# Latent attention in head pairs: PSUM banks assigned by kind of work, weight splitting and quotients moved from VectorE to ScalarE and GpSimd, reciprocals spread over the steps

## The chip, the core and the metric

One core of one Trainium2 chip runs a kernel of two transformer layers (linear attention, mixture of experts, latent attention, a quantised feed-forward). The metric is the device time of one execution in microseconds. TensorE (PE) has its own weight loads (PEld), VectorE is DVE, ScalarE is ACT, GpSimd is POOL, SyncE (SP) issues most DMAs. All engines run their own instruction lists in order and wait for each other on semaphores.

## The reference, cut to the stage that is changed

```python
# _L1_attn_ref: b=2, s=1024 (the shape in use), H=16 heads, NOPE, ROPE, VD = 128, 64, 128, LORA=64
q = (x @ wq).reshape(b, s, H, QH).transpose(0, 2, 1, 3)
kva = x @ wkv_a
ckv, k_pe = (kva[..., :LORA], kva[..., LORA:])
ckv = ckv * rsqrt(mean(ckv * ckv) + EPS) * kv_norm_scale
kv = (ckv @ wkv_b).reshape(b, s, H, NOPE + VD).transpose(0, 2, 1, 3)
k_nope, v = (kv[..., :NOPE], kv[..., NOPE:])
q_pe, k_pe = _rope(q_pe, cos, sin), _rope(k_pe, cos, sin)
scores = einsum('bhqd,bhkd->bhqk', qs, ks_) * QH ** -0.5      # causal
attn = softmax(scores, axis=-1)
out = einsum('bhqk,bhkd->bhqd', attn, v).transpose(0, 2, 1, 3).reshape(b, s, H * VD)
return out @ wo
```

## The kernel before, in words

**What a core holds.** Key and value weights are folded into the query and output weights beforehand, so all heads share one key tile `k_hl` (64 latent rows and 64 rotated rows, 128 x 1024) and one value tile `v_hl` (64 latent columns, 64 columns of ones). Every fp32 operand is split into a high and a low fp32r part (`_hl`), and a product is three matmuls: high by high, high by low, low by high. The PSUM tensor `bank` (`all_bank` in the rows) has eight banks of 128 x 512 fp32.

**Loops.** `phase_attention` (L1230) runs once per batch entry, twice in all. It goes over 8 head pairs n, and within a pair over 10 groups x = 0 to 9. A group is a block i of 256 queries (both heads side by side, 512 columns) and a pair jj of key tiles, jj <= i: block 0 is x=0, block 1 is x=1, 2, block 2 is x=3 to 5, block 3 is x=6 to 9. One pass of the loop over u (L1414), that is one group, is called a step; u counts steps over all pairs. Each engine has its own loop over the same steps.

**A step on TensorE** (L1414 to L1431): first half of the scores of step u+2, one aside item, second half of those scores, an aside item, first half of the values of step u, an aside item, second half of the values, any further item. `scores` (L1358) writes two banks, alternating between banks 0, 1 and 2, 3. `values` (L1382) accumulates over a block; block e uses bank 4 or 5 by turns, and the first values of a block wait until the block before the last has been copied out (`sums_sb`, L1388).

**Aside items** belong mostly to the next pair. A *query* (L1331, Q0 to Q3, one in each of x=0 to 3) is six matmuls that make 128 query rows x 512 tokens. A *piece* (L1346) is the scores of 128 queries of one head against up to 512 keys; VectorE takes its row maximum (`peaks`, L1568), which `spread` (L1574) turns into the diagonal matrix `minus` that the scores subtract. There are three pieces in most steps from x=4 on. All aside items share banks 6 and 7 in turn (`bank_of`, L1305), in the order of one list, so each waits until the reader of the item two places before it is through (`bank_free`, L1321): `by_cos` after a query, `peaks` after a piece. The aside list in x=0 is query, piece, piece; in x=1 query, piece; in x=2 query, piece; in x=3 query, piece, piece.

**What a query needs behind it.** ScalarE swaps halves of the rotated rows (`swap`, L1435, two copies out of PSUM), VectorE multiplies by the cosines (`by_cos`, L1559, out of PSUM into `raw`), GpSimd multiplies the swapped rows by the sines (L1510) and adds (L1513; the two are `rotate`), ScalarE makes the high part (`q_high`, L1450), GpSimd the low part (`q_low`, L1520).

**ScalarE's order in a step** (L1490): swap, `probs` (the exponential, L1457) and `highs` (L1464) of step u+2, `q_high`, and, where a block ends, `sums` (four copies of 64 x 256 out of the value bank, L1475 and L1476). **GpSimd's order** (L1538): `q_low` of the query before, `rotate`, `low` of step u+2 (the low part of the probabilities, L1526). **VectorE's order** (L1616): the readers of the step's aside items (where the step has a query, the first piece goes ahead of it), then the quotients of a block (`divide`, L1589: two reciprocals of 128 x 128, L1596, two products, L1600) in steps 2, 4, 7 and 1 of the next pair, then the splitting of the weights of the pair after next: `weights_high` (L1553) in step 5, `weights_low` (L1557) in step 6. SyncE loads those weights (L1317) when the splitting before is through.

**Opening and last pair.** Before the loop TensorE makes the four queries of pair 0 and 16 of its pieces (L1404 to L1413), and VectorE reads them all and splits the weights of pair 1. In the last pair there are no queries and no pieces of a next pair. The last block's quotient is taken in `phase_output`, which the change does not touch.

Of the kernel before, what the change touches and what calls it, by code (L numbers as in the profile page):

```python
# [13 lines left out]
F32 = mybir.dt.float32  # L14
# [4 lines left out]
ALU = mybir.AluOpType  # L19
# [3 lines left out]
P = 128  # L23
# [1206 lines left out]
def phase_attention(nc, name, bank, cst_turned, turned_loaded, bf, xT, x_hl, wqk_rows, w_raw, w_hl, k_hl, v_hl, oT, last_den):  # L1230
# [28 lines left out]
    DIVIDE_AT = {2: 0, 4: 1, 7: 2, 1: 3}  # L1259
# [12 lines left out]
    order = opening + [item for n in range(PAIRS) for x in range(NG) for item in aside(n, x)]  # L1272
    place = {item: a for a, item in enumerate(order)}
# [9 lines left out]
    with Memory(nc, name) as m:  # L1283
# [10 lines left out]
        rden = m.sb("rden", [P, 2, P])  # L1294
# [16 lines left out]
        with nc.Block() as block:  # L1311
# [8 lines left out]
            def _(pe):  # L1320
                def bank_free(item):  # L1321
                    a = place[item]
                    if a < 2:
                        return
                    kind, n, v = order[a - 2]
                    if kind == "query":
                        pe.wait_ge(raw_sb, n * QC + v + 1)
                    else:
                        pe.wait_ge(peak_sb, n * NP + v + 1)

                def query(item):  # L1331
                    _, n, k = item
                    h, c = chunk(k)
                    bank_free(item)
# [3 lines left out]
                    for xs, ws in ((0, 0), (0, 1), (1, 0)):  # L1338
                        for kc in range(KC):
                            mm = nc.tensor.matmul(bank_of(item), w_hl[:, ws, kc, h * P:(h + 1) * P],  # L1340
# [41 lines left out]
                def values(u, half):  # L1382
# [9 lines left out]
                    out = pv_ps[e % 2].rearrange("p (h m) -> p h m", h=2)[:, :, q0:BW]  # L1392
# [41 lines left out]
            def _(act):  # L1434
                def swap(n, k):  # L1435
                    c = n * QC + k
                    ps = bank_of(("query", n, k))
# [3 lines left out]
                    nc.scalar.copy(swapped[LORA:LORA + 32, c % 2], ps[LORA + 32:P])  # L1441
                    nc.scalar.copy(swapped[LORA + 32:P, c % 2], ps[LORA:LORA + 32]).then_inc(swap_sb, 1)
# [23 lines left out]
                def sums(n, i):  # L1466
# [5 lines left out]
                    for h in range(2):  # L1472
                        half, cols = slice(h * LORA, (h + 1) * LORA), slice(h * BW, (h + 1) * BW)
                        own = last_den[half, :] if e == PAIRS * NB - 1 else den[half, e % 2, :]
                        nc.scalar.copy(own, pv_ps[e % 2][LORA:P, cols])  # L1475
                        done = nc.scalar.copy(oT[half, n, i * BW:(i + 1) * BW], pv_ps[e % 2][0:LORA, cols])  # L1476
# [5 lines left out]
                for k in range(QC):  # L1482
                    q_high(0, k)
                    if k + 2 < QC:
                        swap(0, k + 2)
# [578 lines left out]
```

## Time and profile before

| What | Value |
|---|---|
| Time of three runs | 1497.5, 1510.41 (median), 1512.34 us |
| Profiled execution | 1508.22 us, of which the span from the first to the last instruction is 1506.4 us |
| TensorE clock over the span | 0.924 of full |
| Busy share of the span | PE 83%, POOL 65%, DVE 61%, PEld 59%, ACT 46% |
| First run of the attention stage | from 491 us (first query matmul) to 919 us (last copy of the value sums) |
| Second run of it | from 961 us to 1387 us |

Times inside a trace are microseconds from the start of the span. A timeline row gives start, duration, engine, line, operation, output<-input, shape and count, and in brackets the engine's idle time before it and what ended that. Where a row has a count above one, its duration is the merged stretch. A granted clock of 1.00 is 2.4 GHz and 0.50 is 1.2 GHz.

### The profile page before, as it was taken

How to read it: one execution, taken by the hardware profiler on the slowest of the kernel's cores; microseconds unless marked ns; L12 is line 12 of the kernel's file. 1: busy time of each engine (PE TensorE's matmuls, PEld its weight loads, DVE VectorE, ACT ScalarE, POOL GpSimd, SP SyncE). 2: the span in 40 equal slices, each digit the busy share in tenths (PEclk: the TensorE clock that was granted, in tenths of full speed). 3: DMA queues.
4: the chain of work that ended last, by engine and by line, in shares of the span. 5: the costliest groups of instructions: out<-in, count | busy, mean ns of one | idle time of the engine just before them, and what ended most of it. 6: DMA issues, size and time to landing. Idle time of an engine off the chain costs nothing. (4 is left out here: it accounts for less than half of the span.)

```text
span 1506.4 us, 19134 instructions
## 1 busy us (share of the span) xinstructions
PE 1245.2 (83%) x5880; PEld 883.6 (59%) x5881; DVE 911.9 (61%) x1575; ACT 692.3 (46%) x1183; POOL 984.2 (65%) x688
## 2 busy tenths in 40 slices
PE   6965699999954788988988897688889888988797
PEld 5854455555533456655655576556556556666786
DVE  4578422222217467686768675556867777775557
ACT  3211233333312366556656664255666566657242
POOL 2017588888855577678767755766776677676554
PEclk9976699999985699999999999889999999999899
DMA  9367245555443000000000000000000000001101
GB/s 326 122 181 171 80 79 83 79 81 80 80 77 127 14 1 8 8 8 1 8 8 1 1 1 12 8 8 8 7 1 8 8 1 8 0 1 38 25 8 49
DMA packets 66512, 68.31 MB, mean 45 GB/s; under 512 B 15072, under 2 KB 59680, under 8 KB 66304
## 3 DMA queue, kind: packets, MB, share of 16 engines
q1 hardware_dynamic: 48336, 43.42, 9.8%
q0 software_dynamic: 15168, 20.72, 8.7%
q10 hardware_dynamic: 2928, 3.15, 0.6%
q8 instruction: 44, 0.72, 0.2%
q14 instruction: 36, 0.29, 0.1%
HBM read 46.17 MB, written 21.10 MB: 45 GB/s over the span
## 5 line engine op out<-in xcount | busy, mean ns | idle before, releaser
L1526 POOL TENSOR_TENSOR att_prob_lo<-att_prob,att_prob_hi 128x1024 fp32r<-128x1024 f32 (+1 forms) x160 | 351.8, 2199 | 202.3 <-ACT att_prob_hi L1464 202.3
L1571 DVE TENSOR_REDUCE att_peak<-all_bank 128x1 f32<-128x512 f32 (+3 forms) x384 | 205.8, 552 | 199.8 <-PE all_bank L1355 138.5
L1371 PE MATMUL all_bank<-att_q_hl,sequence_k_hl 128*128 128x512 f32 (+1 forms) x960 | 272.9, 396 | 0.0
L1352 PE MATMUL all_bank<-sequence_k_hl,att_q_hl 128*128 128x512 f32 (+3 forms) x384 | 184.5, 484 | 84.3 <-DVE all_xT L1565 63.0
L1457 ACT ACTIVATE att_prob<-all_bank 128x1024 f32<-128x1024 f32 (+1 forms) x160 | 150.5, 941 | 196.3 <-PE all_bank L1377 165.0
L1394 PE MATMUL all_bank<-att_prob_hi,sequence_v_hl 128*128 128x512 f32 (+1 forms) x640 | 206.0, 403 | 2.3 <-POOL att_prob_lo L1526 2.0
L1371 PEld LDWEIGHTS all_bank<-att_q_hl,sequence_k_hl 128*128 128x128 f32 x960 | 176.8, 199 | 27.9
L1464 ACT CAST att_prob_hi<-att_prob 128x1024 fp32r<-128x1024 f32 (+1 forms) x160 | 153.9, 962 | 5.2
L916 PE MATMUL all_bank<-early_w_gu,moe_xgT 128*128 x316 | 148.8, 553 | 3.5 <-issue 2.4
L1352 PEld LDWEIGHTS all_bank<-sequence_k_hl,att_q_hl 128*128 128x128 f32 x384 | 78.3, 205 | 123.3 <-DVE all_xT L1565 78.1
L881 POOL DMA_INDIRECT sums<-moe_y,early_slot_far x79 | 125.5, 1589 | 36.4 <-issue 18.5
L1340 PE MATMUL all_bank<-sequence_x_hl,sequence_w_hl 128*128 128x512 f32 x384 | 112.4, 432 | 34.0 <-DVE all_xT L1565 26.3
L1394 PE MATMUL all_bank<-att_prob_lo,sequence_v_hl 128*128 128x512 f32 x320 | 121.5, 380 | 0.0
L1377 PE MATMUL all_bank<-att_minus,all_bf 128*128 128x512 bf16 x320 | 120.1, 375 | 0.0
L1394 PEld LDWEIGHTS all_bank<-att_prob_hi,sequence_v_hl 128*128 128x128 f32 x640 | 111.0, 196 | 12.7 <-POOL att_prob_lo L1526 4.1
L1600 DVE TENSOR_TENSOR late_oT<-late_oT,att_rden 128x128 f32<-128x128 f32 x124 | 115.0, 966 | 0.0
L1596 DVE RECIPROCAL att_rden<-att_den 128x128 f32<-128x128 f32 x124 | 108.6, 916 | 10.5 <-ACT late_oT L1476 10.5
L1008 DVE COPY moe_hidT<-all_bank 112x256 f32<-112x256 f32 x79 | 33.6, 425 | 123.6 <-PE all_bank L926 123.6
L1340 PEld LDWEIGHTS all_bank<-sequence_x_hl,sequence_w_hl 128*128 128x128 f32 x384 | 73.7, 198 | 57.8 <-DVE all_xT L1565 35.9
L871 POOL DMA_INDIRECT moe_xg<-x_rows,early_slot_row x79 | 84.2, 1065 | 26.1 <-issue 21.5
L1513 POOL TENSOR_TENSOR all_xT<-all_xT 128x512 f32<-128x512 f32 x64 | 82.3, 1286 | 25.4 <-DVE all_xT L1565 18.0
L935 PE MATMUL all_bank<-early_w_down,moe_hidT 112*128 x316 | 87.3, 399 | 13.6 <-issue 12.2
(246 smaller groups left out, 2197.8 us busy)
## 6 DMA issues: line engine op xcount, KB each, us to landing
sequence_w_raw<-wqk_rows SPq DMA_DIRECT2D x16, 256.0 KB, 2.7
early_w_gu<-in_gate SPq DMA_DIRECT2D x16, 224.0 KB, 5.7
early_w_gu<-in_up SPq DMA_DIRECT2D x16, 224.0 KB, 5.9
early_w_down<-in_down SPq DMA_DIRECT2D x1, 3584.0 KB, 19.4
sums<-early_zero SPq DMA_DIRECT2D x18, 128.0 KB, 3.9
all_xT<-in_xT SPq DMA_DIRECT2D x4, 512.0 KB, 7.6
all_x_tok<-in_x SPq DMA_DIRECT2D x1, 2048.0 KB, 16.2
x_rows<-all_x_tok SPq DMA_DIRECT2D x4, 512.0 KB, 3.0
```

The costliest lines, as they stand in the source:

```text
L881: nc.gpsimd.indirect_dma_start(sums[s], bass.IndirectOffsetOnAxis(slot_far[:, r:r + 1], 0), y[:, s, :], None, bounds_check=last_far, compu ...
L916: mm = nc.tensor.matmul(gu_ps[s], xgT[:, s, k, :], w_gu[:, bass.ds(e * (KC * 2 * I) + k * 2 * I, 2 * I)], start=k == 0, stop=k == KC - 1)
L1340: mm = nc.tensor.matmul(bank_of(item), w_hl[:, ws, kc, h * P:(h + 1) * P], x_hl[:, xs, kc, c * WIDE:(c + 1) * WIDE], start=i == 0, stop=i ...
L1352: mm = nc.tensor.matmul(ps[:, 0:w], q_hl[n % 2][:, 0, h, t * P:(t + 1) * P], k_hl[:, 0, k0:k0 + w], start=True, stop=not diagonal)
L1371: nc.tensor.matmul(ps, k_hl[:, ks, j * P:(j + 1) * P], q_hl[n % 2][:, qs, :, i * BW + q0:(i + 1) * BW], start=g == 0, stop=False)
L1377: mm = nc.tensor.matmul(ps, bf["ones"], minus[:, i, :].rearrange("p (h m) -> p h m", h=2)[:, :, q0:BW], start=False, stop=True)
L1394: mm = nc.tensor.matmul(out, v_hl[:, vs, j, :], part[:, u % 3, half * WIDE:half * WIDE + 2 * w].rearrange("p (h m) -> p h m", h=2), start= ...
L1457: nc.scalar.activation(prob[:, u % 2, 0:w], s_ps[u % 2][:, 0:w], ACT.Exp, scale=SCALE).then_inc(prob_sb, 1)
L1464: nc.scalar.copy(prob_hi[:, u % 3, 0:w], prob[:, u % 2, 0:w]).then_inc(hi_sb, 1)
L1526: nc.gpsimd.tensor_tensor(prob_lo[:, u % 3, 0:w], prob[:, u % 2, 0:w], prob_hi[:, u % 3, 0:w].bitcast(F32), ALU.subtract).then_inc(lo_sb, 1)
L1571: nc.vector.tensor_reduce(peak[:, n % 2, part, t // 2, h, t % 2:t % 2 + 1], bank_of(("piece", n, y))[:, 0:w], AX_X, ALU.max).then_inc(peak ...
L1600: nc.vector.tensor_tensor(own, own, rden[:, half, :], ALU.mult).then_inc(o_sb, 1)
```

## The change

TensorE's aside items no longer share two banks. Queries have bank 5 alone, and each waits for the cosine product of the query before it. Pieces alternate between banks 6 and 7, each waiting for the maximum two pieces before. The value sums have bank 4 alone, so the first values of a block wait for the copies of the block just before. The high part of the weights is made by ScalarE in step 4, the low part by GpSimd in step 5. `divide` is gone: VectorE takes one reciprocal of 128 x 128 in each of steps 1 to 8, and GpSimd one product of 128 x 256 in steps 3, 5, 7 and 9.

```diff
-    DIVIDE_AT = {2: 0, 4: 1, 7: 2, 1: 3}
+    INVERT_AT = {1: (-1, 0), 2: (-1, 1), 3: (0, 0), 4: (0, 1), 5: (1, 0), 6: (1, 1), 7: (2, 0), 8: (2, 1)}
+    PRODUCT_AT = {3: -1, 5: 0, 7: 1, 9: 2}
...
-        rden = m.sb("rden", [P, 2, P])
+        rden = m.sb("rden", [P, 2, BW])
...
-        pv_ps = [bank[:, n, :] for n in (4, 5)]
-        aside_ps = [bank[:, n, :] for n in (6, 7)]
-
-        def bank_of(item):
-            return aside_ps[place[item] % 2]
+        pv_ps, q_ps = bank[:, 4, :], bank[:, 5, :]
+        piece_ps = [bank[:, n, :] for n in (6, 7)]
...
                 def query(item):
-                    bank_free(item)
+                    if n * QC + k:
+                        pe.wait_ge(raw_sb, n * QC + k)
...
                 def piece(item):
-                    bank_free(item)
+                    if n * NP + y >= 2:
+                        pe.wait_ge(peak_sb, n * NP + y - 1)
                     pe.wait_ge(q_hi_sb, n * QC + t // 4 * 2 + h + 1)
-                    ps = bank_of(item)
+                    ps = piece_ps[y % 2]
...
                 def values(u, half):
-                        if jj == 0 and e >= 2:
-                            pe.wait_ge(sums_sb, e - 1)
+                        if jj == 0 and e >= 1:
+                            pe.wait_ge(sums_sb, e)
...
             def _(act):
+                def weights_high(n):
+                    act.wait_ge(w_loaded, 16 * n)
+                    act.wait_ge(q_mm, n * QC)
+                    nc.scalar.copy(w_hl[:, 0], w_raw[:]).then_inc(w_hi_sb, 1)
...
                         q_high(n + 1, x)
                     if x in last_of:
                         sums(n, last_of.index(x))
+                    if x == 4 and n + 2 < PAIRS:
+                        weights_high(n + 2)
...
             def _(pool):
+                def weights_low(n):
+                    pool.wait_ge(w_hi_sb, n)
+                    nc.gpsimd.tensor_tensor(w_hl[:, 1], w_raw[:], w_hl[:, 0].bitcast(F32), ALU.subtract).then_inc(w_sb, 1)
+
+                def product(e):
+                    n, i = divmod(e, NB)
+                    own = oT[:, n, i * BW:(i + 1) * BW]
+                    pool.wait_ge(rden_sb, 2 * (e + 1))
+                    nc.gpsimd.tensor_tensor(own, own, rden[:, e % 2], ALU.mult).then_inc(o_sb, 1)
...
                     if u + AHEAD < STEPS:
                         low(u + AHEAD)
+                    if x == 5 and n + 2 < PAIRS:
+                        weights_low(n + 2)
+                    if x in PRODUCT_AT and n * NB + PRODUCT_AT[x] >= 0:
+                        product(n * NB + PRODUCT_AT[x])
...
             def _(dve):
-                def weights_high(n):
-                def weights_low(n):
-                def divide(n, i):
-                    for half in range(2):
-                        nc.vector.reciprocal(rden[:, half, :], den[:, e % 2, half * P:(half + 1) * P]).then_inc(rden_sb, 1)
-                    for half in range(2):
-                        own = oT[:, n, i * BW + half * P:i * BW + (half + 1) * P]
-                        nc.vector.tensor_tensor(own, own, rden[:, half, :], ALU.mult).then_inc(o_sb, 1)
+                def invert(e, half):
+                    cols = slice(half * P, (half + 1) * P)
                     dve.wait_ge(sums_sb, e + 1)
+                    if e >= 2 and half == 0:
+                        dve.wait_ge(o_sb, e - 1)
+                    nc.vector.reciprocal(rden[:, e % 2, cols], den[:, e % 2, cols]).then_inc(rden_sb, 1)
...
-                weights_high(1)
-                weights_low(1)
...
-                    if x in DIVIDE_AT:
-                    if x == 5 and n + 2 < PAIRS:
-                        weights_high(n + 2)
-                    if x == 6 and n + 2 < PAIRS:
-                        weights_low(n + 2)
+                    if x in INVERT_AT:
+                        i, half = INVERT_AT[x]
+                        if n * NB + i >= 0:
+                            invert(n * NB + i, half)
```

In the opening, `weights_high(1)` stands behind the four `q_high` on ScalarE, and `weights_low(1)` behind the four `q_low` on GpSimd. The readers of the query bank (`swap`, `by_cos`) and of the value bank (`sums`) take the new bank names.

## Rows read from the trace of the kernel before

**Rows 1.** Busy time by stretch: first attention stage, two pairs, two microseconds

```profile
core 0: us, PE busy (x) PEld busy (x) DVE busy (x) ACT busy (x) POOL busy (x), PEclk, DMA share, GB/s
530.00:917.00 387.00, 340.09 (x1596) 234.65 (x1596) 278.25 (x380) 240.86 (x360) 276.19 (x161) 0.97 0.02 4
630.10:681.95 51.85, 45.17 (x215) 31.19 (x213) 38.72 (x52) 32.00 (x49) 37.17 (x23) 0.97 0.02 6
681.95:732.70 50.75, 43.81 (x215) 30.24 (x213) 38.95 (x52) 32.00 (x49) 37.66 (x23) 1.00 0.02 6
758.00:760.00 2.00, 2.00 (x6) 1.10 (x5) 0.00 (x0) 0.62 (x1) 2.00 (x2) 0.50 0.03 8
```

**Rows 2.** TensorE waits, 530:917, then 985:1386 (total us, times, longest)

```profile
PE all_bank L1352 <- DVE all_xT L1565: 24.6, 15, 2.7
PE all_bank L1340 <- DVE all_xT L1565: 12.7, 12, 1.1
PE all_bank L1352 <- DVE att_peak L1571: 8.5, 20, 0.9
...
PE all_bank L1352 <- DVE all_xT L1565: 25.3, 16, 2.7
PE all_bank L1352 <- DVE att_peak L1571: 9.7, 23, 0.9
```

**Rows 3.** Timeline of TensorE in one pair, from its Q0 on

```profile
681.95 1.74 PE L1340 MATMUL all_bank<-sequence_x_hl,sequence_w_hl 128*128 128x512 f32 x6
...
685.90 0.51 PE L1352 MATMUL all_bank<-sequence_k_hl,att_q_hl 128*128 128x512 f32 x1 [0.69 <-DVE all_xT L1565]
...
690.25 0.71 PE L1394 MATMUL all_bank<-att_prob_hi,sequence_v_hl 128*128 128x512 f32 x2
...
693.89 1.66 PE L1340 MATMUL all_bank<-sequence_x_hl,sequence_w_hl 128*128 128x512 f32 x6 [1.09 <-DVE all_xT L1565]
...
699.85 1.65 PE L1340 MATMUL all_bank<-sequence_x_hl,sequence_w_hl 128*128 128x512 f32 x6 [1.15 <-DVE all_xT L1565]
...
702.04 0.71 PE L1394 MATMUL all_bank<-att_prob_hi,sequence_v_hl 128*128 128x512 f32 x2
...
705.73 0.39 PE L1352 MATMUL all_bank<-sequence_k_hl,att_q_hl 128*128 128x256 f32 x1 [2.74 <-DVE all_xT L1565]
```

**Rows 4.** Timeline of GpSimd in the same pair

```profile
691.19 1.29 POOL L1510 TENSOR_TENSOR all_xT<-all_xT,sequence_cst_turned 128x512 f32<-128x512 f32 x1 [0.45 <-ACT all_xT L1442]
693.91 1.29 POOL L1513 TENSOR_TENSOR all_xT<-all_xT 128x512 f32<-128x512 f32 x1 [1.42 <-DVE all_xT L1565]
...
700.28 1.30 POOL L1513 TENSOR_TENSOR all_xT<-all_xT 128x512 f32<-128x512 f32 x1
```

**Rows 5.** Timeline of ScalarE in the same pair

```profile
689.56 0.36 ACT L1476 COPY late_oT<-all_bank 64x256 f32<-64x256 f32 x1
...
701.61 0.62 ACT L1450 CAST att_q_hl<-all_xT 128x512 fp32r<-128x512 f32 x1 [2.42 <-POOL all_xT L1513]
...
703.39 0.36 ACT L1476 COPY late_oT<-all_bank 64x256 f32<-64x256 f32 x1
```

**Rows 6.** Timeline of VectorE in the same pair

```profile
691.21 1.30 DVE L1580 TENSOR_TENSOR att_whole<-att_peak 128x4 f32<-128x4 f32 x1
...
695.42 3.58 DVE L1600 TENSOR_TENSOR late_oT<-late_oT,att_rden 128x128 f32<-128x128 f32 x2
```

**Rows 7.** By line: low query parts (GpSimd), weight parts (VectorE)

```profile
L1520 POOL TENSOR_TENSOR att_q_hl<-all_xT,att_q_hl 128x512 fp32r<-128x512 f32 x64 | 86.1, 1347 | 0.0
...
L1557 DVE TENSOR_TENSOR sequence_w_hl<-sequence_w_raw,sequence_w_hl 128x512 fp32r<-128x512 f32 x14 | 35.2, 2517 | 0.1
```

**Rows 8.** Timeline of the opening, VectorE

```profile
506.12 0.69 DVE L1565 TENSOR_TENSOR all_xT<-all_bank,sequence_cst_turned 128x512 f32<-128x512 f32 x1 [3.15 <-POOL att_q_hl L1520]
```

**Rows 9.** Timeline of the last pair, ScalarE and TensorE

```profile
898.87 0.37 ACT L1475 COPY att_den<-all_bank 64x256 f32<-64x256 f32 x1
...
899.11 0.71 PE L1394 MATMUL all_bank<-att_prob_hi,sequence_v_hl 128*128 128x512 f32 x2
```

More of the change, by code:

```diff
@@ L1271, in phase_attention @@
     opening = [("query", 0, k) for k in range(QC)] + [("piece", 0, y) for y in range(EARLY)]
-    order = opening + [item for n in range(PAIRS) for x in range(NG) for item in aside(n, x)]
-    place = {item: a for a, item in enumerate(order)}
     def at(u):
@@ L1320, in _ @@
             def _(pe):
[L1321 to L1329, printed above, removed]
                 def query(item):
@@ L1436, in swap @@
                     c = n * QC + k
-                    ps = bank_of(("query", n, k))
                     act.wait_ge(q_mm, c + 1)
@@ L1440, in swap @@
                         act.wait_ge(rot_sb, c - 1)
-                    nc.scalar.copy(swapped[LORA:LORA + 32, c % 2], ps[LORA + 32:P])
-                    nc.scalar.copy(swapped[LORA + 32:P, c % 2], ps[LORA:LORA + 32]).then_inc(swap_sb, 1)
+                    nc.scalar.copy(swapped[LORA:LORA + 32, c % 2], q_ps[LORA + 32:P])
+                    nc.scalar.copy(swapped[LORA + 32:P, c % 2], q_ps[LORA:LORA + 32]).then_inc(swap_sb, 1)
+                def weights_high(n):
+                    act.wait_ge(w_loaded, 16 * n)
+                    act.wait_ge(q_mm, n * QC)
+                    nc.scalar.copy(w_hl[:, 0], w_raw[:]).then_inc(w_hi_sb, 1)
                 def q_high(n, k):
@@ L1474, in sums @@
                         own = last_den[half, :] if e == PAIRS * NB - 1 else den[half, e % 2, :]
-                        nc.scalar.copy(own, pv_ps[e % 2][LORA:P, cols])
-                        done = nc.scalar.copy(oT[half, n, i * BW:(i + 1) * BW], pv_ps[e % 2][0:LORA, cols])
+                        nc.scalar.copy(own, pv_ps[LORA:P, cols])
+                        done = nc.scalar.copy(oT[half, n, i * BW:(i + 1) * BW], pv_ps[0:LORA, cols])
                     done.then_inc(sums_sb, 1)
@@ L1485, in _ @@
                         swap(0, k + 2)
+                weights_high(1)
                 probs(0)
@@ L1535, in _ @@
                     q_low(0, k)
+                weights_low(1)
                 low(0)
@@ L1564, in by_cos @@
                         dve.wait_ge(q_lo_sb, c - 1)
-                    nc.vector.tensor_tensor(raw[:, c % 2], bank_of(("query", n, k)), cos[:, cols], ALU.mult
+                    nc.vector.tensor_tensor(raw[:, c % 2], q_ps, cos[:, cols], ALU.mult
                                             ).then_inc(raw_sb, 1)
@@ L1570, in peaks @@
                     dve.wait_ge(max_mm, n * NP + y + 1)
-                    nc.vector.tensor_reduce(peak[:, n % 2, part, t // 2, h, t % 2:t % 2 + 1], bank_of(("piece", n, y))[:, 0:w],
+                    nc.vector.tensor_reduce(peak[:, n % 2, part, t // 2, h, t % 2:t % 2 + 1], piece_ps[y % 2][:, 0:w],
                                             AX_X, ALU.max).then_inc(peak_sb, 1)
@@ L1587, in spread @@
                                                    ALU.mult, ALU.mult).then_inc(minus_sb, 1)
-                def divide(n, i):
-                    e = n * NB + i
+                def invert(e, half):
+                    cols = slice(half * P, (half + 1) * P)
                     dve.wait_ge(sums_sb, e + 1)
-                    for half in range(2):
-                        if e:
-                            dve.wait_ge(o_sb, 2 * (e - 1) + half + 1)
-                        nc.vector.reciprocal(rden[:, half, :], den[:, e % 2, half * P:(half + 1) * P]).then_inc(rden_sb, 1)
-                    for half in range(2):
-                        own = oT[:, n, i * BW + half * P:i * BW + (half + 1) * P]
-                        dve.wait_ge(rden_sb, 2 * e + half + 1)
-                        nc.vector.tensor_tensor(own, own, rden[:, half, :], ALU.mult).then_inc(o_sb, 1)
+                    if e >= 2 and half == 0:
+                        dve.wait_ge(o_sb, e - 1)
+                    nc.vector.reciprocal(rden[:, e % 2, cols], den[:, e % 2, cols]).then_inc(rden_sb, 1)
                 def beside(item):
@@ L1622, in _ @@
                         beside(item)
-                    if x in DIVIDE_AT:
-                        i = DIVIDE_AT[x]
-                        if i < NB - 1:
-                            divide(n, i)
-                        elif n:
-                            divide(n - 1, i)
-                    if x == 5 and n + 2 < PAIRS:
-                        weights_high(n + 2)
-                    if x == 6 and n + 2 < PAIRS:
-                        weights_low(n + 2)
+                    if x in INVERT_AT:
+                        i, half = INVERT_AT[x]
+                        if n * NB + i >= 0:
+                            invert(n * NB + i, half)
 def phase_output(nc, name, bank, cst, power, x_tok, oT, last_den, vo, b, latent_of=None, x_hl=None, quantised=None):
```

9 lines of the change are left out of this document (2 added, 7 removed).

## The prediction

> **What bounds the kernel now.** I read the busy time by stretch first. In the middle of the first attention stage TensorE is busy 340 of 387 us at a clock of 0.97; GpSimd has 276, VectorE 278, ScalarE 241 [rows 1]. So TensorE sets the pace, and what can be won there is its idle time, 47 us in this stretch and about as much in the second stage. Next I read the waits: pieces held by `by_cos` (L1565), 24.6 + 25.3 us; queries held by it, 12.7 us and the same row once more in the second stage; pieces held by `peaks` (L1571), 8.5 + 9.7 us. That is 93.5 us, nearly all of TensorE's idle time in both stages, and every one of these waits is `bank_free`, a wait for one of the two shared aside banks [rows 2].
>
> The timeline says which. In the pair that begins at 681.95 TensorE stops four times in steps 0 to 3: 0.69 us (second own piece), 1.09 us (Q2), 1.15 us (Q3) and 2.74 us (second piece of step 3), 5.67 us in all [rows 3]. The piece waits stand behind a query's chain of swap and cosine product only because they share its bank. The waits on `peaks` come in the later steps: 18.2 us over 14 pairs that have a successor, 1.3 us a pair [rows 2].
>
> **The sum is made per pair**, for those 14 pairs (seven in each stage), against the profiled 1508.2 us, which is 2.2 us under the median of the runs.
>
> *Banks, steps 0 to 3.* With a bank for queries, the 0.69 and the 2.74 us go entirely: those pieces then wait only for a maximum long taken. Q3 waits for the cosine product of Q2, as it does now; but that product stood behind `divide`, whose products alone took 3.58 us there [rows 6]. With one reciprocal in its place the 1.15 us go. Q2 waits for the cosine product of Q1, behind the first piece of step 1 and its `spread`; as the pair reaches that piece 0.69 us sooner, and the small maximum in front of the cosine product was held for 1.30 us, to the end of GpSimd's sine product (691.19 + 1.29 = 692.48) [rows 4, 6], I take the 1.09 us as gone too. The held operation now starts before the sine product, not beside it.
>
> *One bank for the value sums.* This adds a wait in front of each block. What is queued behind it is everything on TensorE. Steps 0 to 1: the copies of block 0 end at 689.92 [rows 5]; their chain is swap, cosine, add, `q_high` of Q0, unchanged; TensorE would reach the values of block 1 at 690.25 - 0.69 = 689.56 [rows 3]. New wait 0.44 us with 0.08 us for the signal. Steps 2 to 3: here `sums` stands behind `q_high` of Q2 on ScalarE, which sat idle 2.42 us for GpSimd's add and began at 701.61; the four copies end at 703.75 [rows 5]. The add began at 700.28 at the end of a GpSimd queue that had one hole of 1.42 us, the wait for the cosine product of Q1 [rows 4]. If that product comes 1.3 us sooner, the copies end at 702.45. TensorE would reach the values of block 2 at 702.04 - 0.69 - 1.09 - 1.15 + 0.44 = 699.55 [rows 3]. So it waits to 702.53: 2.98 us, a new stall nearly as long as the longest one removed. Its bounds: 4.2 us if the add comes no sooner than now, 2.9 us if the whole hole closes. At the other two block ends (steps 5 and 9) no query stands before the copies; four of 0.37 us [rows 9] end beside the scores and pieces that TensorE does in between, and I count nothing (1.5 us each without that cover).
>
> Steps 0 to 3 then give 5.67 - 0.44 - 2.98 = 2.25 us a pair, between 1.0 and 2.4.
>
> *Work off VectorE, steps 4 to 9.* VectorE loses eight products of 128 x 128, one weight copy and one weight subtraction of 2.5 us [rows 6, 7] and keeps its reciprocals, one a step. So the 1.3 us of waits on `peaks` mostly go. I take 1.0 us, between 0.5 and 1.3.
>
> *What arrives elsewhere.* GpSimd gets per pair one subtraction of 128 x 512, 1.35 us by the same shape in `q_low` [rows 7], and four products of half that width, between 0.7 and 1.35 us each by the same row; I take 0.75. That is 4.3 us on 37.7 of 50.75 [rows 1]; with a pair of 47.5 us GpSimd would be 88% busy. Three of the products and the subtraction stand in steps 3 to 7, behind the chain of Q2 and where GpSimd has holes; the fourth, in step 9, stands just before the sine product of Q0, which waits for the swap anyway. I count nothing for all of these; without that cover the step 9 product costs its 0.75 us in every pair. ScalarE gets a copy of 128 x 512, 0.62 us by `q_high` [rows 5], in step 4, where it has no query; nothing. SyncE's weight load moves one step earlier with the split and stays hidden.
>
> *Opening.* Q0 to Q3 of pair 0 now go one behind the other's cosine product. Before, the cosine product of Q3 came 3.84 us (3.15 + 0.69) after that of Q2, held by GpSimd [rows 8]. Now a lap is two swap copies, a cosine product of 0.69 and a query of 1.65 (at 2.4 GHz) [rows 3, 8], with copies no dearer than `q_high`'s 0.62 [rows 5] 3.6 us, or 5.2 us with the query at 1.2 GHz. Between 0 and 4 us a stage; I take 2, so +4 in all.
>
> *Last pair.* Without queries TensorE runs faster than ScalarE's copies: block 1's begin at 898.87 and take four times 0.37, to 900.35, while the values of block 2 began at 899.11 [rows 9]. With one bank that is a wait of 1.3 us; block 3 has the same and blocks 0 and 1 small ones. I take 2.9 us a stage, so +5.8.
>
> The sum: 14 x (2.25 + 1.0) = 45.5 us off, 9.8 us on. 1508.2 - 35.7 = 1472.5 us, and with the 2.2 us to the median about **1475 us**. I leave the clock as it is: a pair at 0.97 takes 1.1 us more than one at 1.00 [rows 1], and a gap of about 3 us in step 3 remains.
>
> **A rule weighed against the row.** The 1.30 us that a maximum over four columns took, ending with GpSimd's sine product, show VectorE held by GpSimd [rows 4, 6]. The Trainium skill ("SBUF — State Buffer", section "SBUF: two separate sides") says that the two share one port pair as an exclusive lock, for the whole instruction; this row agrees. By that rule more GpSimd work can hold `spread`, and with it the cosine product of Q1, as long as now: this is the first rival below, and it gives its time. A second rule speaks against the move: "GPSIMD Engine Reference", section "Engine selection", puts elementwise work with two inputs on VectorE, GpSimd being about twice as slow. Here the subtraction took 2.52 us on VectorE against 1.35 on GpSimd at the same shape [rows 7], so the measurement decides the other way.
>
> **Rivals.**
> *The value bank gives most of it back.* `spread` is held as before, the add of Q2 comes at 700.28, and the step 3 stall is 4.2 us. Steps 0 to 3 give 1.0, the rest 0.5: 14 x 1.5 - 9.8 = 11 us off, **1499 us**. For it: the row of 1.30. Against: the piece arrives earlier than the sine product starts.
> *More than forecast.* GpSimd's holes close, all waits on `peaks` go, and the remaining gap no longer lowers the clock: 2.4 + 1.3 + 1.1 = 4.8 us a pair, 14 x 4.8 - 9.8 = 57 us off, **1453 us**. For it: one pair ran at 1.00 with a gap of 2.74 us. Against: after the same kind of gap another pair ran at 1.2 GHz (758 to 760) [rows 1].
> *Slower: GpSimd's queue starts each pair late.* The product of step 9 stands ahead of Q0's sine product. If it takes much longer than half a `q_low`, being held by VectorE, every later operation to the add of Q2 slips, and TensorE pays it in step 3, us for us. It decides where the slip passes 3.25 - 9.8 / 14 = 2.55 us. At 4 us, 14 x 1.45 = 20 us on, **1531 us**. For it: VectorE's products took 1.8 us each against GpSimd [rows 6]. Against: GpSimd's own rows hardly vary (1.29, 1.29, 1.30) [rows 4].
> *It doesn't do what it says:* the pieces still wait, now for `peaks`, and the step 3 stall replaces the rest, **1508 us**. Against: 18 us of waits on `peaks` beside 75 on `by_cos` [rows 2].
>
> **How the numbers follow.** Forecast 0.55, value bank 0.17, more 0.14, slower 0.07, no effect 0.07. About 1% (15 us) is what a measurement of this kernel can tell from no change. Forecast and "more" are faster by that, and about a third of the value bank case: 0.75. The rest of that case, no effect, and a little of the slower one are within 1%: 0.18. Slower 0.07. The range takes in "more" and the value bank case: 1448 to 1502 us.
>
> **What would show it.** Right: waits of L1352 and L1340 on `by_cos` below 10 us over both stages; a new wait of TensorE's values (L1394 before) on `sums`, about 3 us once a pair in step 3 and 0.4 us in step 1; pairs of 47 to 49 us; GpSimd near 88% in a pair; VectorE down by some 10 us a pair; slower openings. Wrong: a step 3 stall over 4 us, queries still held by more than 0.5 us, products on GpSimd above 1.4 us, or a clock below 0.95 in the stage.

## The result, and the profile after

The changed kernel takes 1458.12 us (median of 4 runs, 1448.77 to 1465.05) against 1511.38 us for the kernel before (median of 4): a ratio of 0.9656, 95% interval 0.9586 to 0.9726. Its profiled execution is the slowest of the four, 1465.05 us with a span of 1463.3; against the profiled 1508.2 us of before that is 43 us, and the steps below are held against these 43 us (forecast: 35.7).

The first part of the page after, busy time by engine. VectorE had 911.9 us before and GpSimd 984.2:

```profile
PE 1235.1 (84%) x5880; PEld 894.6 (61%) x5881; DVE 744.3 (51%) x1423; ACT 700.5 (48%) x1197; POOL 1043.6 (71%) x764
```

The waits of TensorE after, first stage from its first query on, answer to [rows 2]; columns as there. L1327 is the query, L1340 the piece, L1382 the values:

```profile
PE all_bank L1382 <- POOL att_prob_lo L1531: 23.3, 8, 3.4
...
PE all_bank L1382 <- ACT late_oT L1468: 7.1, 9, 1.3
PE all_bank L1327 <- DVE all_xT L1566: 6.5, 3, 2.4
...
PE all_bank L1340 <- DVE att_peak L1572: 2.6, 4, 1.6
```

No piece waits for a cosine product any more (24.6 us before), and no query does outside the opening, where the three waits of 6.5 us stand; the four waits on `peaks` stand there too. What is new are waits of the values: one of 2.5 to 3.4 us in each of the seven pairs that make a next pair's queries, and ten smaller ones.

Busy time after, by stretch: a pair from Q0 to Q0, then three stretches within it around its long wait. They answer to [rows 1]:

```profile
core 0: us, PE busy (x) PEld busy (x) DVE busy (x) ACT busy (x) POOL busy (x), PEclk, DMA share, GB/s
672.18:720.18 48.00, 44.01 (x216) 31.79 (x213) 26.63 (x42) 32.56 (x50) 41.17 (x28) 0.96 0.02 6
...
688.50:692.88 4.38, 1.03 (x10) 0.84 (x8) 0.29 (x1) 2.21 (x6) 4.24 (x4) 0.99 0.00 0
692.88:696.00 3.12, 3.12 (x8) 2.38 (x9) 1.82 (x3) 2.68 (x4) 2.98 (x3) 0.50 0.03 5
696.00:700.00 4.00, 4.00 (x20) 2.60 (x19) 2.53 (x5) 2.15 (x3) 4.00 (x4) 0.97 0.01 2
```

The pair takes 48.00 us where 51.85 and 50.75 stood. TensorE idles 48.00 - 44.01 = 3.99 us in it (6.94 in the pair before at clock 1.00). Right behind the long wait the granted clock is 0.50, the lower of its two levels, for 3.1 us.

The same pair on TensorE (its queries and its two waits), which answers to [rows 3]:

```profile
672.18 1.74 PE L1327 MATMUL all_bank<-sequence_x_hl,sequence_w_hl 128*128 128x512 f32 x6
...
676.74 1.74 PE L1327 MATMUL all_bank<-sequence_x_hl,sequence_w_hl 128*128 128x512 f32 x6
...
680.32 0.71 PE L1382 MATMUL all_bank<-att_prob_hi,sequence_v_hl 128*128 128x512 f32 x2 [0.63 <-ACT late_oT L1468]
680.87 0.39 PE L1382 MATMUL all_bank<-att_prob_lo,sequence_v_hl 128*128 128x512 f32 x1
...
682.52 1.74 PE L1327 MATMUL all_bank<-sequence_x_hl,sequence_w_hl 128*128 128x512 f32 x6
...
687.09 1.72 PE L1327 MATMUL all_bank<-sequence_x_hl,sequence_w_hl 128*128 128x512 f32 x6
...
692.88 1.19 PE L1382 MATMUL all_bank<-att_prob_hi,sequence_v_hl 128*128 128x512 f32 x2 [3.35 <-POOL att_prob_lo L1531]
```

Two waits, 3.98 us, where four took 5.67. ScalarE just ahead of the long wait, which answers to [rows 5]:

```profile
690.59 0.62 ACT L1442 CAST att_q_hl<-all_xT 128x512 fp32r<-128x512 f32 x1 [2.31 <-POOL all_xT L1508]
691.23 0.37 ACT L1467 COPY att_den<-all_bank 64x256 f32<-64x256 f32 x1
...
692.37 0.36 ACT L1468 COPY late_oT<-all_bank 64x256 f32<-64x256 f32 x1
```

`q_high` of Q2 waits 2.31 us for GpSimd's add, the copies of the value sums stand behind it and end at 692.73, and the values start 0.15 us later. The profile puts this wait down to a low part of GpSimd that ends at 692.85; but that one belongs to the next step, and the low part that these values need ended at 686.65 (684.26 + 2.39). Which of the two engines holds them is what the first experiment asks.

### The profile page after: what moved, and what is told of

The parts are those of the page before. It is cut to its first block and busy times, and to the rows that moved or that the text cites. A ratio compares the mean times of both kernels' runs of the same rounds, so it can differ in the third digit from the quotient of the medians.

```text
span 1463.3 us, 19068 instructions
## 1 busy us (share of the span) xinstructions
PE 1235.1 (84%) x5880; PEld 894.6 (61%) x5881; DVE 744.3 (51%) x1423; ACT 700.5 (48%) x1197; POOL 1043.6 (71%) x764
## 5 line engine op out<-in xcount | busy, mean ns | idle before, releaser
L1531 POOL TENSOR_TENSOR att_prob_lo<-att_prob,att_prob_hi 128x1024 fp32r<-128x1024 f32 (+1 forms) x160 | 346.2, 2164 | 118.6 <-ACT att_prob_hi L1456 118.5
L1572 DVE TENSOR_REDUCE att_peak<-all_bank 128x1 f32<-128x512 f32 (+3 forms) x384 | 209.3, 551 | 245.4 <-PE all_bank L1343 175.8
L1359 PE MATMUL all_bank<-att_q_hl,sequence_k_hl 128*128 128x512 f32 (+1 forms) x960 | 267.9, 390 | 0.0
L1382 PE MATMUL all_bank<-att_prob_hi,sequence_v_hl 128*128 128x512 f32 (+1 forms) x640 | 212.9, 415 | 61.4 <-POOL att_prob_lo L1531 46.7
L1340 PE MATMUL all_bank<-sequence_k_hl,att_q_hl 128*128 128x512 f32 (+3 forms) x384 | 174.3, 457 | 5.7 <-DVE att_peak L1572 5.3
L1382 PEld LDWEIGHTS all_bank<-att_prob_hi,sequence_v_hl 128*128 128x128 f32 x640 | 113.1, 201 | 78.0 <-POOL att_prob_lo L1531 51.7
L1327 PE MATMUL all_bank<-sequence_x_hl,sequence_w_hl 128*128 128x512 f32 x384 | 117.1, 443 | 20.3 <-DVE all_xT L1566 12.6
L1596 DVE RECIPROCAL att_rden<-att_den 128x128 f32<-128x128 f32 x124 | 115.7, 939 | 26.8 <-POOL late_oT L1526 26.8
L1382 PE MATMUL all_bank<-att_prob_lo,sequence_v_hl 128*128 128x512 f32 x320 | 124.8, 390 | 0.0
L1327 PEld LDWEIGHTS all_bank<-sequence_x_hl,sequence_w_hl 128*128 128x128 f32 x384 | 75.9, 200 | 38.8 <-DVE all_xT L1566 16.6
L1505 POOL TENSOR_TENSOR all_xT<-all_xT,sequence_cst_turned 128x512 f32<-128x512 f32 x64 | 83.9, 1311 | 19.0 <-ACT all_xT L1429 19.0
L1566 DVE TENSOR_TENSOR all_xT<-all_bank,sequence_cst_turned 128x512 f32<-128x512 f32 x64 | 44.0, 688 | 98.4 <-ACT all_xT L1429 95.0
```

The costliest lines, as they stand in the source:

```text
L1327: mm = nc.tensor.matmul(q_ps, w_hl[:, ws, kc, h * P:(h + 1) * P], x_hl[:, xs, kc, c * WIDE:(c + 1) * WIDE], start=i == 0, stop=i == 3 * KC ...
L1340: mm = nc.tensor.matmul(ps[:, 0:w], q_hl[n % 2][:, 0, h, t * P:(t + 1) * P], k_hl[:, 0, k0:k0 + w], start=True, stop=not diagonal)
L1359: nc.tensor.matmul(ps, k_hl[:, ks, j * P:(j + 1) * P], q_hl[n % 2][:, qs, :, i * BW + q0:(i + 1) * BW], start=g == 0, stop=False)
L1382: mm = nc.tensor.matmul(out, v_hl[:, vs, j, :], part[:, u % 3, half * WIDE:half * WIDE + 2 * w].rearrange("p (h m) -> p h m", h=2), start= ...
L1531: nc.gpsimd.tensor_tensor(prob_lo[:, u % 3, 0:w], prob[:, u % 2, 0:w], prob_hi[:, u % 3, 0:w].bitcast(F32), ALU.subtract).then_inc(lo_sb, 1)
L1572: nc.vector.tensor_reduce(peak[:, n % 2, part, t // 2, h, t % 2:t % 2 + 1], piece_ps[y % 2][:, 0:w], AX_X, ALU.max).then_inc(peak_sb, 1)
```

## The experiments

All ratios are to the kernel before, measured on the same chip; the changed kernel stands at 0.966.

**1. The copies ahead of the rounding (e1_sums_first).** On ScalarE, after `highs`:

```diff
-                    if made:
-                        q_high(n + 1, x)
                     if x in last_of:
                         sums(n, last_of.index(x))
+                    if made:
+                        q_high(n + 1, x)
```

> The changed kernel with one order turned round on ScalarE: where a block ends, the four copies of the value sums go ahead of q_high instead of behind it. Nothing is left out. Theory S (the stall of step 3, 3.35 us in every pair, is the one value bank, held because the copies wait behind q_high for GpSimd's add): the stalls of step 3 and step 1 fall to below 1 us together, the pair goes from 48.0 to about 44.5 us, and the kernel from 0.966 to about 0.935 of the time before. Rival P (as the row names it, TensorE waits there for GpSimd's low part of the probabilities): the stall stays near 3.3 us and the time at 0.966. Rival Q (GpSimd is the bound behind it): the stall goes, but new waits of 1 to 2 us for the low part stand in steps 4 to 6, and the pair stays at 46 to 47 us, the kernel at about 0.95.

Measured: 1429.65 us, ratio 0.9458 (0.9427 to 0.9489). One pair, by stretch:

```profile
664.75:710.75 46.00, 42.76 (x216) 30.70 (x213) 28.32 (x42) 32.37 (x50) 41.27 (x28) 1.00 0.02 6
```

TensorE in it, the third query and the values of step 3:

```profile
676.00 1.66 PE L1327 MATMUL all_bank<-sequence_x_hl,sequence_w_hl 128*128 128x512 f32 x6 [1.39 <-DVE all_xT L1566]
...
682.97 0.70 PE L1382 MATMUL all_bank<-att_prob_hi,sequence_v_hl 128*128 128x512 f32 x2
```

VectorE ahead of that query:

```profile
673.60 1.75 DVE L1585 SCALAR_TENSOR_TENSOR att_minus<-all_bf,att_whole 128x512 bf16<-128x512 bf16 x1
675.26 0.68 DVE L1566 TENSOR_TENSOR all_xT<-all_bank,sequence_cst_turned 128x512 f32<-128x512 f32 x1
```

Two lines of ScalarE's order end the 3.35 us (the row at 682.97 shows no wait), so the copies held the values and not the low part that the profile names. No stretch at half clock is left: the pair's clock is 1.00, and TensorE's busy time falls from 44.01 to 42.76 us. That is the larger part of the 2.0 us by which the pair is shorter; its idle time falls by 0.75 us only (3.99 to 3.24), because other waits came in the stall's place. The pair (46.00 us) and the time are therefore those of rival Q and not of theory S, though only one wait on a low part is there, of 0.49 us; the values of step 6 wait 1.31 us for ScalarE's copies, and Q2 waits 1.39 us for the cosine product of Q1, which stands behind `spread`. That operation took 1.75 us: GpSimd's sine product (673.50, 1.30 us) ran until 674.80, and `spread` ended 0.55 us later. In the changed kernel, where it began ahead of GpSimd's sine product (at 681.02), it took 0.69 us. The Trainium skill ("SBUF — State Buffer", section "SBUF: two separate sides") has the two engines hold one port pair in turn; the row at 673.60 agrees with it.

**2. The new banks alone (e2_banks_only).** Weights and quotients stay on VectorE as before (the edit in short):

```diff
-    INVERT_AT = {...}; PRODUCT_AT = {...}
+    DIVIDE_AT = {2: 0, 4: 1, 7: 2, 1: 3}
...
-weights_high on act, weights_low and product on pool
+weights_high, weights_low and divide on dve, where before.py has them
```

> The changed kernel's banks alone: quotients and weight splitting go back to VectorE as before. Theory: without the work taken off VectorE the cosine product of Q2 again stands behind the quotients, so Q3 still waits about 1.1 us, the copies end later, the step 3 stall is 4 us or more and the waits on the maxima stay at 1.3 us a pair; what the banks win in a pair (about 1 us) is lost in openings and last pairs. Time 0.99 to 1.00 of before. Rival (the banks are the larger part): 0.975 or less.

Measured: 1483.63 us, ratio 0.9833 (0.9813 to 0.9854): more gain than the theory had (0.99 to 1.00), less than its rival (0.975). Waits of TensorE, first stage (L1381 is the values, L1339 the piece here), and then two pairs by stretch:

```profile
PE all_bank L1381 <- POOL att_prob_lo L1512: 21.4, 8, 3.0
PE all_bank L1339 <- DVE att_peak L1557: 13.5, 21, 1.6
```

```profile
671.41:721.49 50.08, 44.94 (x215) 31.37 (x213) 34.96 (x52) 32.03 (x49) 37.78 (x23) 0.97 0.02 6
721.49:770.31 48.82, 43.10 (x215) 30.44 (x213) 34.01 (x52) 31.94 (x49) 38.03 (x23) 1.00 0.02 6
```

The banks clear the waits on cosine products with VectorE still doing all its work; the 1.09 and 1.15 us before Q2 and Q3 shrink to 0.28 us before Q3, and the stall of the values is 3.0 us where 4 were expected. The waits on `peaks` stay, 1.2 and 1.8 us in these two pairs. The half-clock stretch comes in every second pair here.

**3. The new placement alone (e3_work_only).** Banks as before (the edit in short):

```diff
-pv_ps, q_ps, piece_ps = banks 4, 5, (6, 7)
+pv_ps = banks (4, 5); aside_ps = banks (6, 7) by turns, with bank_free
```

> The changed kernel's work placement alone: the banks of the kernel before, quotients and weights as after. Theory: Q3's 1.15 us and the 1.3 us of waits on the maxima go, the step 3 piece still waits for the cosine product of Q3 but about 1.2 us less long; no new stall of the values, no cost in the opening or the last pair: 2.4 us and more a pair, some 34 to 45 us in all, 0.97 to 0.978 of before, thus most of the gain. Rival (banks and work each give half): 0.985.

Measured: 1490.41 us, ratio 0.9874 (0.9854 to 0.9894): less gain than the theory had, and close to the rival's 0.985. One pair, by stretch, and its longest wait on TensorE (L1354 is the piece here, L1581 the cosine product):

```profile
677.00:728.12 51.12, 45.50 (x215) 32.04 (x213) 27.86 (x42) 32.54 (x50) 40.60 (x28) 0.93 0.02 6
```

```profile
700.50 0.58 PE L1354 MATMUL all_bank<-sequence_k_hl,att_q_hl 128*128 128x256 f32 x1 [3.99 <-DVE all_xT L1581]
```

The waits on `peaks` and the one before Q3 are gone, but the piece of step 3 waits 3.99 us instead of 2.74. It starts 23.50 us after Q0, where it started 23.78 us after it before [rows 3]: the cosine product of Q3 hangs on the chain over GpSimd and ScalarE, which moved by 0.28 us only, and TensorE merely gets there sooner. The pair's clock is 0.93. The two halves give 1.7% and 1.3%; their sum of 2.9% lies within the interval of the whole change (2.7 to 4.1%), so nothing shows that one half helps the other.

**4. Two banks for the opening's queries (e4_opening).**

```diff
+        def q_bank(n, k):
+            return bank[:, 4 + k % 2, :] if n == 0 else q_ps
```

> The changed kernel, but the four queries of the opening take two banks by turns (the value bank is free until the loop). Theory: the opening's query cost, measured as 0.8 and 3.0 us in the two profiles' stages, goes: 4 us in all, 0.963 of before where the changed kernel has 0.966, which is less than the runs scatter; the trace shows it, first query to the first query of pair 1 in about 32 us where the changed kernel has 33.7 and 34.9. Rival (the opening is held by GpSimd's chain of four rotations whatever the banks): 33.5 us and more stay.

Measured: 1456.88 us, ratio 0.9647 (0.9625 to 0.9669), which the times cannot tell from the changed kernel. In the traces the two openings (first query to the first query of the next pair) take 32.34 and 30.74 us instead of 33.74 and 34.89: 5.5 us, against the rival that GpSimd's chain holds the opening. In the kernel before they took 32.91 and 31.87, so the changed kernel had lost 3.85 us there.

**5. Edits 1 and 4 together, and the cosine product first in step 1 (e5_three_edits).** The third edit:

```diff
-                    if items and items[0][0] == "query":
+                    if items and items[0][0] == "query" and x != 1:
                         items[0:2] = items[1::-1]
```

> The changed kernel with three edits: the copies of the value sums ahead of the rounding of the next queries on ScalarE (as in the run e1_sums_first), the opening's four queries in two banks by turns (as in e4_opening), and in step 1 of a pair VectorE multiplies query 1 by the cosines before it takes that step's maximum and spreads it. Theory S (the value bank's and the query bank's waits are what is left, and they sit in order behind other work): the wait of query 2 that e1 showed (1.39 us a pair) goes, since its product by the cosines then ends some 1.7 us sooner; a pair falls from 46.0 to 44.6 to 45.2 us, the openings give 5 us, and the time is 1405 to 1418 us, 0.930 to 0.938 of the kernel before. Rival G (GpSimd, 41.3 us busy of the 46.0 in e1, is the bound of the pair by now): its queue runs later against TensorE as the pair shrinks, the values wait longer on the low parts (0.49 and 1.0 us in e1), and the pair stays above 45.5 us: 1422 to 1428 us, by the openings alone.

Measured: 1422.21 us, ratio 0.9418 (0.9394 to 0.9443), the best of all. A pair by stretch, and TensorE's waits in one pair (L1332 is the query, L1387 the values):

```profile
654.57:699.98 45.41, 42.80 (x212) 30.64 (x213) 27.42 (x42) 32.43 (x50) 41.75 (x28) 1.00 0.03 7
```

```profile
669.16 1.66 PE L1332 MATMUL all_bank<-sequence_x_hl,sequence_w_hl 128*128 128x512 f32 x6 [0.15 <-DVE all_xT L1571]
...
672.20 0.70 PE L1387 MATMUL all_bank<-att_prob_hi,sequence_v_hl 128*128 128x512 f32 x2 [0.66 <-ACT late_oT L1473]
...
681.18 0.73 PE L1387 MATMUL all_bank<-att_prob_hi,sequence_v_hl 128*128 128x512 f32 x2 [0.49 <-POOL att_prob_lo L1536]
...
686.21 0.70 PE L1387 MATMUL all_bank<-att_prob_hi,sequence_v_hl 128*128 128x512 f32 x2 [1.30 <-ACT late_oT L1473]
```

The 1.39 us before Q2 are gone, but the pair came down by 0.6 us only, and 45.4 us lies just above theory S. Half of the gain went into the wait of step 3 (0.66 us, where e1 shows none). GpSimd's two longest waits in a pair, 0.46 and 2.63 us, stand at its end, and up to step 6 it runs almost without a gap, so rival G has its part. Neither theory held whole: 1422 us is the edge of rival G's time, with a pair between the two bands.

**6. and 7. Quotients back, weights back (e6_quotients_back, e7_weights_back),** each alone in the changed kernel (the edits in short):

```diff
-INVERT_AT, PRODUCT_AT, invert on dve, product on pool
+DIVIDE_AT, divide on dve                                    # e6
...
-weights_high on act at x == 4, weights_low on pool at x == 5
+weights_high, weights_low on dve at x == 5, 6               # e7
```

> The changed kernel with the quotients put back on VectorE as before (two reciprocals and two products in one go, after the peaks of steps 1, 2, 4 and 7); banks and weight splitting as changed. Theory P (a VectorE item costs what the piece or query behind it waits for): by the waits of e2_banks_only 0.28 us before query 3 and 0.35 us behind the quotients of step 4 come back, and a little of the wait on the value sums goes: 0.3 to 0.7 us a pair, 4 to 10 us, 1462 to 1468 us. Rival B (the cost goes with VectorE's busy time): half of the 25 us that separate e2_banks_only from the changed kernel, 1470 us or more. Rival G (GpSimd is the bound): the 3 us a pair that GpSimd gives back make it faster than the changed kernel, below 1455 us.

> The changed kernel with the splitting of the weights put back on VectorE as before (both halves, after the peaks of steps 5 and 6); banks and quotients as changed. Theory P: by the waits of e2_banks_only the pieces behind the two halves wait 0.55 and 0.31 us again: 0.9 us a pair, 12 us, 1468 to 1473 us. Rival B (the cost goes with VectorE's busy time, which here has spread items only): less than 6 us, under 1464 us. Rival G (GpSimd is the bound): 1.3 us a pair of GpSimd's time come back, and the kernel is faster than the changed one, below 1455 us.

Measured: 1476.12 us, ratio 0.9763 (0.9730 to 0.9796), and 1471.39 us, ratio 0.9723 (0.9686 to 0.9760). The intervals from one Q0 to the next are 49.19 and 48.98 us on average, against 48.15 in the changed kernel, so both moves pay. For the weights only the traces show it; in the times their interval overlaps that of the changed kernel (0.9586 to 0.9726). GpSimd is not the bound of the changed kernel: giving it less made nothing faster. With the weights back the time lies where theory P had it, and the waits of pieces on `peaks` rise from 2.6 to 7.5 us in the first stage, 0.8 us a pair. With the quotients back the waits are those of theory P (0.28 us before Q3, 0.36 us behind step 4, 3.01 us in step 3), yet the time is 8 us above it, where rival B had it. Rival B's reason fails with the weights, for which it had less than 1464 us; what the quotients cost beyond their waits is busy time of TensorE. Two pairs of each, by stretch, first e6:

```profile
674.84:723.51 48.67, 44.39 (x212) 31.32 (x213) 31.00 (x50) 32.61 (x50) 39.02 (x24) 0.96 0.02 6
624.84:674.84 50.00, 45.74 (x211) 32.22 (x213) 31.39 (x50) 32.61 (x50) 38.50 (x24) 0.93 0.03 6
```

```profile
575.73:626.26 50.53, 45.82 (x211) 32.49 (x213) 29.49 (x44) 32.01 (x49) 40.14 (x27) 0.93 0.02 6
...
675.50:723.63 48.13, 42.74 (x211) 30.70 (x213) 29.55 (x44) 31.91 (x49) 40.54 (x27) 1.00 0.03 6
```

In e6 the two pairs idle 4.28 and 4.26 us; TensorE's busy time, 1.35 us apart, makes the whole difference. In e7 (second fence) two pairs of one and the same order are 2.40 us apart, with 4.71 and 5.39 us idle: busy time 45.82 against 42.74. The half-clock stretch is longer, shorter or missing, and it weighs as much as the waits.

**8. The copies between exponential and rounding (e8_sums_before_highs),** on top of e5:

```diff
                         probs(u + AHEAD)
+                    if x in last_of:
+                        sums(n, last_of.index(x))
+                    if u + AHEAD < STEPS:
                         highs(u + AHEAD)
-                    if x in last_of:
-                        sums(n, last_of.index(x))
```

> The kernel of the run e5_three_edits, with the four copies of a block's value sums between the exponentials and their rounding on ScalarE instead of behind both (1.05 us sooner). Theory S (the order on ScalarE sets the wait on the value bank): of the waits before the values that e5 shows in a pair, 0.66 us in step 3 and 1.30 us in step 6, some 1.5 us go: a pair of 45.4 us becomes 44.0 to 44.4 us, and the time 1403 to 1410 us. Rival G (GpSimd, 41.7 of 45.4 us busy and without a gap from step 0 to step 6 in e5, is the bound of that stretch): the roundings are late by 1.5 us in these steps, GpSimd's low parts and with them the values are late in their place, and the time stays within 1417 to 1430 us.

Measured: 1445.18 us, ratio 0.9567 (0.9530 to 0.9604): 23 us slower than e5, worse than either theory had it. GpSimd at the end of a pair whose next Q0 starts at 618.22, in e8, and then in e5, where it starts at 699.98:

```profile
620.22 2.40 POOL L1537 TENSOR_TENSOR att_prob_lo<-att_prob,att_prob_hi 128x1024 fp32r<-128x1024 f32 x1 [4.75 <-ACT att_prob_hi L1461]
...
623.27 1.30 POOL L1511 TENSOR_TENSOR all_xT<-all_xT,sequence_cst_turned 128x512 f32<-128x512 f32 x1
```

```profile
699.93 2.40 POOL L1536 TENSOR_TENSOR att_prob_lo<-att_prob,att_prob_hi 128x1024 fp32r<-128x1024 f32 x1 [2.63 <-ACT att_prob_hi L1461]
...
703.00 1.29 POOL L1510 TENSOR_TENSOR all_xT<-all_xT,sequence_cst_turned 128x512 f32<-128x512 f32 x1
```

The waits on ScalarE's copies did go (0.16 us is left in step 3). But at the end of a pair the copies now keep back a rounding, GpSimd idles 4.75 us for it instead of 2.63, and its sine product of Q0 starts 5.05 us after Q0 instead of 3.02. TensorE pays for it before Q2 and Q3 of that pair:

```profile
628.67 1.65 PE L1332 MATMUL all_bank<-sequence_x_hl,sequence_w_hl 128*128 128x512 f32 x6 [0.59 <-DVE all_xT L1572]
...
634.79 1.65 PE L1332 MATMUL all_bank<-sequence_x_hl,sequence_w_hl 128*128 128x512 f32 x6 [1.30 <-DVE all_xT L1572]
```

The cosine products that they wait for stand behind a `swap`, and on ScalarE the `swap` stands behind `q_high` of the query before, which waits for GpSimd's add (1.48 and 2.18 us). The pair takes 47.64 us instead of 45.41: idle time is up by 1.33 us (2.61 to 3.94), busy time by 0.90 (42.80 to 43.70). So GpSimd starts each pair late, as in the prediction's third rival, but with another cause, and TensorE pays before the queries and not in step 3.

**9. The old order in every second pair (e9_odd_pairs_late),** on top of e5:

```diff
+                    if made and n % 2:
+                        q_high(n + 1, x)
                     if x in last_of:
                         sums(n, last_of.index(x))
-                    if made:
+                    if made and n % 2 == 0:
                         q_high(n + 1, x)
```

> The kernel of the run e5_three_edits, where in the odd-numbered pairs alone the next queries' rounding stands ahead of the copies of the value sums on ScalarE again, as in the changed kernel: within one execution every second pair has the long wait of step 3. Theory C (the stall brings a stretch at half the granted clock behind it, and its price is its own length plus 1.2 to 3 us): granted clock 1.00 in the even pairs and 0.93 to 0.97 in the odd ones, TensorE busy 42.8 us in the even and 44.0 to 45.8 us in the odd, pairs of 45.4 and 47.8 to 49.5 us. Rival (the clock falls by the state of the chip, whatever the waits are): both kinds of pairs show the same clock, and they differ by the 2 to 3 us of the waits alone.

Measured: 1436.1 us in a single run. Four pairs in a row, by stretch, from n = 1 to n = 4:

```profile
566.09:614.42 48.33, 44.01 (x212) 31.58 (x213) 27.11 (x42) 32.59 (x50) 41.48 (x28) 0.96 0.02 6
614.42:659.80 45.38, 42.83 (x212) 30.64 (x213) 27.47 (x42) 32.35 (x50) 41.72 (x28) 1.00 0.03 7
659.80:709.40 49.60, 45.30 (x212) 32.49 (x213) 27.10 (x42) 32.56 (x50) 41.48 (x28) 0.93 0.02 6
709.40:754.77 45.37, 42.81 (x211) 30.64 (x213) 27.42 (x42) 32.37 (x50) 41.70 (x28) 1.00 0.02 6
```

The clock follows the stall from pair to pair in one execution: 0.96, 1.00, 0.93, 1.00. The pairs with the stall idle 1.75 us more on average (4.32 and 4.30 against 2.55 and 2.56) and are busy 1.2 and 2.5 us longer for the same matmuls. Theory C holds in this execution, and its rival fails; the length of the half-clock stretch is not fixed by the stall, though (0.96 and 0.93 here, and in e7 a stall of 3.65 us in the pair at 1.00).

## Why the prediction was right, point by point

**The time.** 1458.12 us measured, 1475 forecast, range 1448 to 1502: the sign and the mechanism hold, the gain is 17 us larger. Of these, some 7.5 us stand in the profiled executions (43.2 against 35.7); the rest is how these stand to their medians, which I had carried over from the kernel before (2.2 us), and which for the changed kernel is 7 us the other way.

**The pair.** Forecast 3.25 us off. The twelve intervals from one Q0 to the next (six a stage) went from 52.2 to 48.15 us on average: 4.06 off. 12 x 0.81 = 9.7 us is more than the 7.5 us; the first query comes 2.04 us later than before (493.30 against 491.26), after code that is unchanged, and the other terms held.

*Idle time: right, slightly too much.* In the pair of the rows TensorE idles 2.95 us less (6.94 to 3.99); forecast 3.25. Steps 0 to 3: the four waits went as foreseen, Q2 and Q3 included. The new ones are 0.63 and 3.35 us (forecast 0.44 and 2.98), so these steps gave 1.69 us and not 2.25. The copies ended 20.55 us after Q0 (forecast 20.50); but TensorE was at the values after 17.35 us instead of 17.60, and the signal took 0.15 us, not 0.08. Steps 4 to 9: no wait on `peaks` is left in this pair, 1.3 us and not 1.0.

*What was mis-sized: the sum took the waits at the idle time that their rows show, and TensorE's busy time as given.* That time fell as well, from 45.4 to 44.2 us on average over the twelve (45.17 in a pair of [rows 1], 44.01 after): the 1.2 us by which the pair was mis-sized. The clock is the small part of it. Against pairs at 1.00 (43.81 us in [rows 1], 42.76 in e1) the half-clock stretch costs 45.4 - 43.8 = 1.6 us a pair before and 44.2 - 42.8 = 1.4 after (an estimate: the changed kernel has no pair at 1.00, and e1's stands in for it); so "I leave the clock as it is" held on balance. The large part, 1.05 us, is there at full clock: where TensorE waits less often it is busy less, for the same matmuls. That is a pattern over kernels (the last section has six), which no run tests by itself. Rows of the changed kernel's pair suggest why: six matmuls in a row take 1.74 us, one alone 0.39, so each further one adds 0.27 and some 0.12 us of the last stand alone where a wait follows. By that a wait removed gives its idle time and a little more; seven waits became two.

*What it saw and did not price.* It had the stall of 2.98 us and its cause, `sums` behind `q_high`, and counted its length. The stall also costs 1.2 to 2.5 us of busy time by the half clock behind it (experiments 1 and 9), and two lines of ScalarE's order remove both: 1458.1 - 1429.7 = 28 us, beside the 53 us of the whole change.

**Opening and last pair.** Forecast +4 us for the openings; 0.83 and 3.02 are 3.85. For the last pair, 2.9 us on and 3.25 off a stage leave 0.35 us off; from its Q0 to the copies of the last sums it took 79.3 and 79.1 us before and 78.8 in both stages after.

**What arrives elsewhere.** GpSimd is busy 41.17 of 48.00 us, 86% (forecast 88%); the products took 0.74 us each in this pair (0.75). VectorE is down 12 us a pair (forecast 10). Experiment 7 shows no cost of the 1.3 us that the weights take on GpSimd.

**The rivals.** "The value bank gives most back": no; the add came with the forecast to 0.1 us. Its row was not typical: in the kernel before, the small maximum took 0.16 us in 23 cases of 32 and 1.30 in four. In the changed kernel it took 0.52 to 0.75 us in 26 of 32; in the pair of the rows it took 0.53, to 680.99, with GpSimd's low part of Q0 ending at 680.97. So it is held more often now; here it stands ahead of the sine product, as forecast, and the shorter hold left Q2 without a wait. "More than forecast": its 1453 us lie nearer to the measured time, but of its three parts only the waits on `peaks` came; the half-clock stretch stayed, and the size came from the busy time instead. "Slower": not here; e8 brought the late start of GpSimd's queue about by accident. "Doesn't do what it says": no, by the waits above.

**What should show it.** Waits on cosine products outside the opening: none. New waits of 3 and 0.4 us: 3.35 and 0.63. Pairs of 47 to 49 us: 48. All as written.

## What to carry to other kernels

A bank with one user makes the engine that empties it part of the critical path: put the copies that free it ahead of anything on that engine that waits for a third one, but not so early that they hold back what feeds the busiest helper. Price a long stall of TensorE as its length plus the half-clock stretch behind it, read from a pair of the same kernel that shows one, and every wait a little above its idle time (by the pattern over kernels below, which is not tested). And where an operation may be held by another engine, put what TensorE waits for in front of it.

## What was not expected of the hardware

- The half-clock stretch behind the same stall has different lengths in one execution: in e7, with one order, pairs with a stall of 3.4 to 3.7 us ran at 0.93, 0.97 and 1.00. What decides between them stays open.
- The name behind a wait can be a coincidence: the values' 3.35 us were put down to a GpSimd operation that ended 0.03 us before they began, and went when ScalarE's order changed.
- At clock 1.00 a pair's busy time on TensorE goes with the number of its waits: 43.81 us with seven (the kernel before), 43.70 with six (e8), 43.10 with five (e2), 42.80 with four (e5), 42.76 with three (e1), 42.74 with three (e7, which idles 2.2 us more than e1). From seven to three that is some 0.25 us a wait beyond the idle time shown, in uneven steps, and about twice what the rows of single matmuls explain. No run tests why.
